# One sign operation of 1536 columns in place of three of 512, in the attention stage of a decoder layer

## The chip, the cores and the metric

The kernel runs on one core of a Trainium2 chip. The metric is the device time of one execution in microseconds, the median of several runs.

## The reference

The reference is a decoder layer of batch 4, 512 tokens and width 512, in fp32: x + attention(layernorm(x)), and then x + ffn(layernorm(x)). The attention has 32 query heads and 8 key and value heads of 16 columns. Its four linear maps use only the signs of their weights, with a scale for each output row.

The part that the change touches is the weights of the ffn. Each of its three matrices is made of a weight w and a mean m:

```
d = w - base
coeff = jnp.mean(jnp.abs(d))
return base + coeff * jnp.sign(d)
```

So three things are needed of each difference d: its sign, element by element, and the mean of its magnitudes over the whole matrix. The ffn is then silu(x W1) * (x W3) times W2, with 1792 inner columns.

## The kernel before

The core runs in stages. The first projects the first batch's tokens. The second, from about 85 to 450 us, is the attention, and all that can be done beside it stands in it too. The third makes the ffn's weights and transposes them, and the last, from about 545 us, is the ffn.

**The attention stage** is written as 32 groups g (4 batches x 8 key heads) of 4 slices kt (tiles of 128 keys), 128 slices in all, numbered 4g + kt. Each engine has its own function for a slice, and the order of the work is written out by hand: on each engine the instructions run in the order of the program, and semaphores tie the engines together.

In a slice TensorE (pe_slice) does, in this order: two of the slice's four transposed score tiles (shifted_scores, L1554), one pair of natural scores of a later group for the maxima (scores, L1538), the piece beside if there is one, another pair of natural scores, the other two transposed scores, and the matmuls that weigh the values with the exps of the slice before (weigh_values, L1564). In slices of kt 1 a transposition of the maxima (L1544) follows.

The transposed scores go to a ring of three PSUM banks (RING3). Each user of the ring waits (ring_free) until the user three places before it has been read: for a score, until its exp is done.

The piece beside (function beside) is work of the next batch: a transposition of tokens in slices 0 to 3 of a batch's 32, pieces of projections (L1445 and L1446) in slices 5, 6, 8, 9, 11, 12, 14, 15, 17, 18, 20 and 21, and a transposition of values in 19. In the first batch all of these come two slices later. In the last batch slices 22, 24, 26 and 28 hold output projections instead.

ScalarE (act_slice) does for each slice: four exps (L1018), with the read of the piece beside between the second and the third (for a projection, L925); in slices of kt 0 a copy of the weighed values (copy_u, L1038), which waits for the value matmuls; and then, from a table by slice, its part of the ffn's weights.

VectorE takes the maxima of the natural scores (L1188), and turns them into a shift (L1196, L1198) that goes into the query slots by DMA (load_shift, L517) before the next group's transposed scores.

**The ffn's weights.** They have 14 tiles e, each with three parts k of 128 x 512 (w1, w3, w2). Buffers wn (three of them) hold w and mn (two) the mean. For tile e, DIFF_AT[e] = 8, 16, ... 112 is the slice in which GpSimd takes the first difference, in place in wn (difference, L799, semaphore fd_ok); the other two come in the next two slices. SIGN_LAG is 2: ScalarE takes the sign of part k in slice DIFF_AT[e] + 2 + k (L1029, semaphore fsgn_ok), into sgn, an int8 tile [128, 14, 3, 512], and the magnitudes of part k, with their sum, in slice DIFF_AT[e] + 5 + k (L1031, semaphore facc_ok), in place in wn. The sync engine loads the next tile into a buffer wn when fsgn_ok and facc_ok have both reached the count of the tile that was in it (load_difference). The signs are next read after slice 123, by full_weights.

So the signs of a tile stand in slices DIFF_AT[e] + 2, + 3 and + 4, which are slices of kt 2, 3 and 0.

Of the kernel before, what the change touches and what calls it, by code (L numbers as in the profile page):

```python
# [11 lines left out]
ACT = mybir.ActivationFunctionType  # L12
# [49 lines left out]
def positive(eng, sem, value):  # L62

    if not isinstance(value, int) or value > 0:
        eng.wait_ge(sem, value)
# [32 lines left out]
def decoder_layer(nc, x, q_w, q_s, k_w, k_s, v_w, v_s, o_w, o_s, w1, m1, w2, m2, w3, m3, out):  # L98
    ctx = ExitStack()

    def sem(name):
        return ctx.enter_context(nc.semaphore(name))
# [47 lines left out]
    wn, mn = stage[0::2], stage[1::2]  # L150
# [40 lines left out]
    with ExitStack() as scope:  # L191
        sb = region(scope)
        sb("below_sgn", [P, 2144])
        sgn = sb("sgn", [P, IT, 3, HID], I8)
# [65 lines left out]
    fd_ok = sem("fd_ok")  # L260
    fsgn_ok = sem("fsgn_ok")
# [119 lines left out]
    def beside(g, kt):  # L381

        b, at = g // KV_HEADS + 1, 4 * (g % KV_HEADS) + kt
        if b == BATCH:
            return ("project", PROJECT_AT.index(at)) if at in PROJECT_AT else None
        at -= LATER[b]
        if XT_AT <= at < XT_AT + KT:
            return "xT", b, at - XT_AT
        for i in range(len(ITEMS)):
            if 0 <= at - ITEM_AT[i] < 2:  # L390
                return "item", b, i, at - ITEM_AT[i]
        if at == VT_AT:
            return "vT", b
        return None
# [12 lines left out]
    def ring_bank(user):  # L407
        return RING3[ring_place[user] % len(RING3)]

    def score_number(g, kt, j):  # L410
        return 16 * g + 4 * kt + J_ORDER.index(j)
# [483 lines left out]
    def _(act):  # L895
# [89 lines left out]
        def beside_out(user):  # L985

            kind, b, *which = user
            bank = ring_bank(user)
            if kind == "xT":
                kt = which[0]  # L990
                act.wait_ge(xT_ok, 4 * b + kt + 1)
                nc.scalar.activation(xn[:, :, kt * P:(kt + 1) * P], BANK[bank].rearrange("p (t c) -> p t c", c=P),
                                     ACT.Copy).then_inc(xe_ok, 1)
            elif kind == "item":
                scale_item(b, which[0], bank, which[1])
            elif kind == "vT":
                values_out(b, bank)


        def hi_attended(b, kt):  # L1000
            act.wait_ge(aT_ok, 4 * b + kt + 1)
            positive(act, o_mm, 4 * b)
            nc.scalar.activation(ah[:, kt, :], an[:, kt, :], ACT.Copy).then_inc(ah_ok, 1)
# [6 lines left out]
        def act_slice(g, kt):  # L1010

            for j in J_ORDER:
                if j == J_ORDER[2] and beside(g, kt):
                    beside_out(beside(g, kt))
                act.wait_ge(t_mm, score_number(g, kt, j) + 1)
                if j == 0:
                    positive(act, pv_mm, 4 * g + kt - 3)
                nc.scalar.activation(probs[kt][:, j, :], BANK[ring_bank(("score", g, kt, j))], ACT.Exp,  # L1018
                                     scale=HEAD_DIM ** -0.5).then_inc(exp_ok, 1)
            if kt == 0 and g > 0:  # L1020
                copy_u(g - 1)
            k = 4 * g + kt - SLICES * (BATCH - 1) - ATTENDED_AT - 1
            if 0 <= k < KT:
                hi_attended(0, k)
            for e in range(IT):
                k = 4 * g + kt - DIFF_AT[e] - SIGN_LAG
                if 0 <= k < 3:
                    act.wait_ge(fd_ok, 3 * e + k + 1)
                    nc.scalar.activation(sgn[:, e, k, :], wn[e % 3][:, k, :], ACT.Sign).then_inc(fsgn_ok, 1)  # L1029
                if 3 <= k < 6:  # L1030
                    nc.scalar.activation(wn[e % 3][:, k - 3, :], wn[e % 3][:, k - 3, :], ACT.Abs,  # L1031
                                         accum_out=dsum[:, k - 3, e:e + 1]).then_inc(facc_ok, 1)

        def copy_u(g):
            act.wait_ge(pv_mm, 4 * g + 4)
            if g >= 2:
                act.wait_ge(u_out[g % 2], 16 * (g // 2))
            nc.scalar.activation(u_sb[g % 2][:], BANK[6], ACT.Copy).then_inc(u_ok, 1)  # L1038

        for g in range(GROUPS):  # L1040
            for kt in range(TT):
                act_slice(g, kt)
# [692 lines left out]
```

## Time and profile before

| | us |
|---|---|
| median of 3 runs | 998.81 |
| lowest and highest of them | 993.24 and 1002.25 |
| the profiled execution | 1002.4 |
| its span in the profile | 1000.6 |

The span reaches from the first to the last instruction; the 1.8 us between it and the execution's time lie around it. In the rows below, PE is TensorE's matmuls, PEld its weight loads, DVE VectorE, ACT ScalarE, POOL GpSimd, and SPq the sync engine's queue that issues the DMAs. "L1029" is line 1029 of the kernel. A row in the order of time merges neighbouring instructions of one line and says how many there are (x2), so its length is that of the group. In brackets stands how long the engine sat idle before it, and which instruction ended that. A weight load's idle time is not a stall of TensorE where matmuls run meanwhile.

### The profile page before, as it was taken

How to read it: one execution, taken by the hardware profiler on the slowest of the kernel's cores; microseconds unless marked ns; L12 is line 12 of the kernel's file. 1: busy time of each engine (PE TensorE's matmuls, PEld its weight loads, DVE VectorE, ACT ScalarE, POOL GpSimd, SP SyncE). 2: the span in 40 equal slices, each digit the busy share in tenths (PEclk: the TensorE clock that was granted, in tenths of full speed). 3: DMA queues.
4: the chain of work that ended last, by engine and by line, in shares of the span. 5: the costliest groups of instructions: out<-in, count | busy, mean ns of one | idle time of the engine just before them, and what ended most of it. 6: DMA issues, size and time to landing. Idle time of an engine off the chain costs nothing.

```text
span 1000.6 us, 14963 instructions
## 1 busy us (share of the span) xinstructions
PE 958.1 (96%) x5030; PEld 624.2 (62%) x5030; DVE 712.1 (71%) x948; ACT 553.4 (55%) x1078; POOL 304.7 (30%) x312
## 2 busy tenths in 40 slices
PE   7899999999999998987999999999999999999997
PEld 6544434443344433333678888888888888888886
DVE  6778898889888897866955588655886558854443
ACT  5468889889988997955842322423223332232220
POOL 4864666467546413445011111011110111101110
PEclk9979999999999998989999999999999999999999
DMA  6435655465545565623830002310023100220001
GB/s 193 122 109 175 206 162 167 138 209 160 165 130 181 164 208 171 202 68 114 278 125 24 1 1 84 124 50 0 0 84 124 49 0 0 84 84 1 0 0 43
DMA packets 75662, 105.06 MB, mean 105 GB/s; under 512 B 9944, under 2 KB 33496, under 8 KB 75608
## 3 DMA queue, kind: packets, MB, share of 16 engines
q1 hardware_dynamic: 74776, 103.26, 32.9%
q0 software_dynamic: 448, 0.46, 0.2%
q8 instruction: 29, 0.48, 0.2%
q10 hardware_dynamic: 384, 0.66, 0.2%
q14 instruction: 25, 0.20, 0.1%
HBM read 74.59 MB, written 28.05 MB: 103 GB/s over the span
## 4 chain that ended last, share of the span: by engine, by line
PE 81%; DVE 6%; ACT 3%; DMA 3%; POOL 3%; issue 3%; SPq 1%; ACTq 0%; DVEq 0%; POOLq 0%
PE psum L1660 15%; PE psum L1661 15%; PE psum L1662 15%; PE psum L1564 9%; PE psum L1554 8%; PE psum L1538 6%; PE psum L1445 3%; DVE nmx L1188 2%; PE psum L1446 2%; PE psum L1650 2%; PE psum L1575 2%; PE psum L1576 1%; ACT probs L1018 1%; DMA q_slot<-shift 1%; PE psum L1434 1%
## 5 line engine op out<-in xcount | busy, mean ns | idle before, releaser
L1188 DVE TENSOR_REDUCE nmx<-psum 128x2 f32<-128x1024 f32 x256 | 304.6, 1220 | 61.0 <-PE psum L1538 58.9
L1018 ACT ACTIVATE probs<-psum 128x512 f32<-128x512 f32 x512 | 270.8, 602 | 47.5 <-PE psum L1554 45.9
L879 POOL CAST dh<-w2T 128x512 fp32r<-128x512 f32 (+1 forms) x56 | 50.7, 906 | 425.9 <-PE psum L1662 393.7
L1660 PE MATMUL psum<-fxh,wh 128*128 128x512 f32 x448 | 175.1, 391 | 2.2 <-DVE wl L1368 2.2
L1661 PE MATMUL psum<-fxl,wh 128*128 128x512 f32 x448 | 175.2, 391 | 0.0
L1662 PE MATMUL psum<-fxh,wl 128*128 128x512 f32 x448 | 174.9, 390 | 0.0
L1554 PE MATMUL psum<-q_slot,k_slot 50*128 50x512 f32 x512 | 151.3, 478 | 15.0 <-ACT probs L1018 5.9
L1554 PEld LDWEIGHTS psum<-q_slot,k_slot 50*128 50x128 f32 x512 | 65.3, 189 | 132.1 <-ACT probs L1018 62.5
L1564 PE MATMUL psum<-probs,v_slot 128*32 128x512 f32 x1024 | 139.8, 619 | 0.0
L1375 DVE TENSOR_TENSOR gate<-gate,psum 128x512 f32<-128x512 f32 x56 | 38.4, 686 | 133.9 <-PE psum L1662 131.6
L1076 ACT ACTIVATE hh<-gate 128x512 fp32r<-128x512 f32 x56 | 35.4, 632 | 162.0 <-DVE gate L1375 162.0
L1073 ACT ACTIVATE gate<-psum 128x512 f32<-128x512 f32 x56 | 33.5, 598 | 164.3 <-PE psum L1662 164.2
L1538 PE MATMUL psum<-k_slot,q_slot 48*128 48x512 f32 x512 | 105.2, 442 | 4.5 <-DVE nmx L1188 3.3
L1660 PEld LDWEIGHTS psum<-fxh,wh 128*128 128x128 f32 x448 | 84.5, 189 | 20.8 <-issue 2.8
L1662 PEld LDWEIGHTS psum<-fxh,wl 128*128 128x128 f32 x448 | 84.5, 189 | 17.7
L1661 PEld LDWEIGHTS psum<-fxl,wh 128*128 128x128 f32 x448 | 84.4, 188 | 17.7
L1660 PE MATMUL psum<-dh,hh 128*128 128x512 f32 x224 | 88.2, 394 | 0.1
L1661 PE MATMUL psum<-dl,hh 128*128 128x512 f32 x224 | 88.2, 394 | 0.0
L1662 PE MATMUL psum<-dh,hl 128*128 128x512 f32 x224 | 87.1, 389 | 0.0
L1538 PEld LDWEIGHTS psum<-k_slot,q_slot 48*128 48x128 f32 x512 | 49.5, 189 | 28.6 <-DVE nmx L1188 15.0
L1377 DVE TENSOR_TENSOR hl<-gate,hh 128x512 fp32r<-128x512 f32 x56 | 38.8, 692 | 39.8 <-ACT hh L1076 39.8
L799 POOL TENSOR_TENSOR stage<-stage 128x512 f32<-128x512 f32 x42 | 53.2, 1280 | 12.5 <-DMA stage<-in_L_ffn_mean_w_dram 12.5
(134 smaller groups left out, 1337.3 us busy)
## 6 DMA issues: line engine op xcount, KB each, us to landing
stage<-in_L_ffn_mean_w_dram SPq DMA_DIRECT2D x84, 256.0 KB, 3.8
q_slot<-q_stack SPq DMA_DIRECT2D x180, 64.0 KB, 2.3
stage<-in_L_ffn_w_dram SPq DMA_DIRECT2D x42, 256.0 KB, 3.8
weighted_values<-u_sb SPq DMA_DIRECT2D x32, 256.0 KB, 2.4
k_slot<-k_stack SPq DMA_DIRECT2D x60, 96.0 KB, 2.4
an<-weighted_values SPq DMA_DIRECT2D x16, 256.0 KB
al<-reciprocals SPq DMA_DIRECT2D x16, 256.0 KB
x<-_attn_hidden_states_dram SPq DMA_DIRECT2D x8, 512.0 KB, 4.2
```

Source lines behind the costliest of these rows:

```text
L799: nc.gpsimd.tensor_tensor(wn[e % 3][:, k, :], wn[e % 3][:, k, :], mn[e % 2][:, k, :], ALU.subtract).then_inc(fd_ok, 1)
L879: nc.gpsimd.tensor_copy(dh[parity][:], w2T[:, bass.ds(src, 1), :].rearrange("p o c -> p (o c)")).then_inc(dh_ok, 1)
L1018: nc.scalar.activation(probs[kt][:, j, :], BANK[ring_bank(("score", g, kt, j))], ACT.Exp, scale=HEAD_DIM ** -0.5).then_inc(exp_ok, 1)
L1188: v.tensor_reduce(column, pair, AX.X, ALU.max, negate=True).then_inc(s_max, 1)
L1375: v.tensor_tensor(gate[:], gate[:], BANK[UP], ALU.mult).then_inc(h_ok, 1)
L1377: v.tensor_tensor(hl[p][:], gate[:], hh[p][:].bitcast(FP32), ALU.subtract).then_inc(hl_ok, 1)
L1538: last = mm(BANK[2 * jj + h], q_slot[s][rows, jj, q * P:(q + 1) * P], k_slot[s][rows, :], start=True, stop=True)
L1554: mm(BANK[ring_bank(("score", g, kt, j))], k_slot[s][rows, kt * P:(kt + 1) * P], q_slot[s][rows, jj, :], start=True, stop=True).then_inc(t ...
L1564: last = mm(psum[32 * j:32 * j + 32, 6, :], v_slot[g % V_SLOTS][:, kt, :], probs[kt][:, j, :], start=(kt == 0), stop=(kt == TT - 1))
L1660: mm(o, lhs_hi, rhs_hi, start=first, stop=False)
L1661: mm(o, lhs_hi, rhs_lo, start=False, stop=False)
L1662: return mm(o, lhs_lo, rhs_hi, start=False, stop=final)
```

## The change

In act_slice the sign of part k is no longer taken in slice DIFF_AT[e] + 2 + k. In slice DIFF_AT[e] + 4, where k is 2, one operation takes the signs of all three parts, 1536 columns of each partition. It waits until all three differences are done, which is the count that the third sign waited for, and it adds 3 to fsgn_ok at once. The magnitudes stay where they were.

```diff
             for e in range(IT):
                 k = 4 * g + kt - DIFF_AT[e] - SIGN_LAG
-                if 0 <= k < 3:
-                    act.wait_ge(fd_ok, 3 * e + k + 1)
-                    nc.scalar.activation(sgn[:, e, k, :], wn[e % 3][:, k, :], ACT.Sign).then_inc(fsgn_ok, 1)
+                if k == 2:
+                    act.wait_ge(fd_ok, 3 * (e + 1))
+                    nc.scalar.activation(sgn[:, e, :, :], wn[e % 3][:], ACT.Sign).then_inc(fsgn_ok, 3)
                 if 3 <= k < 6:
                     nc.scalar.activation(wn[e % 3][:, k - 3, :], wn[e % 3][:, k - 3, :], ACT.Abs,
                                          accum_out=dsum[:, k - 3, e:e + 1]).then_inc(facc_ok, 1)
```

## Rows read from the trace of the kernel before

**Rows 1.** The page, busy time, share of the span and instructions of each engine.

```profile
PE 958.1 (96%) x5030; PEld 624.2 (62%) x5030; DVE 712.1 (71%) x948; ACT 553.4 (55%) x1078; POOL 304.7 (30%) x312
```

**Rows 2.** Line 1029: durations, first and last start.

```profile
L1029 ACT ACTIVATE sgn<-stage x42: 619/632/662, 90.6 to 424.4; 128x512 int8<-128x512 f32 x42
```

**Rows 3.** Stretches: length, busy PE, PEld, DVE, ACT, POOL, then clock, DMA share, GB/s.

```profile
85.00:340.00 255.00, 248.97 (x1614) 110.87 (x1611) 217.37 (x236) 229.64 (x474) 146.50 (x138) 1.00 0.55 168
340.00:450.00 110.00, 99.35 (x561) 38.51 (x558) 87.09 (x95) 89.35 (x183) 38.90 (x38) 0.93 0.53 162
```

**Rows 4.** Waits from 85 to 450 us: us in total, times, longest.

```profile
PEld psum L1554 <- ACT probs L1018: 55.0, 98, 1.7
```

**Rows 5.** ScalarE in order of time, slices 99 to 101.

```profile
368.17 2.06 ACT L1018 ACTIVATE probs<-psum 128x512 f32<-128x512 f32 x4
370.09 0.65 ACT L1029 ACTIVATE sgn<-stage 128x512 int8<-128x512 f32 x1
370.77 2.06 ACT L1018 ACTIVATE probs<-psum 128x512 f32<-128x512 f32 x4
372.98 0.60 ACT L1038 ACTIVATE u_sb<-psum 128x512 f32<-128x512 f32 x1
373.48 0.62 ACT L1029 ACTIVATE sgn<-stage 128x512 int8<-128x512 f32 x1
374.00 2.05 ACT L1018 ACTIVATE probs<-psum 128x512 f32<-128x512 f32 x4
```

**Rows 6.** TensorE in the same slices.

```profile
371.85 1.06 PE L1564 MATMUL psum<-probs,v_slot 128*32 128x512 f32 x8
...
374.64 0.18 PEld L1554 LDWEIGHTS psum<-q_slot,k_slot 50*128 50x128 f32 x1 [0.49 <-ACT probs L1018]
...
375.07 1.06 PE L1564 MATMUL psum<-probs,v_slot 128*32 128x512 f32 x8
```

**Rows 7.** TensorE, a projection piece beside: behind copy and third sign; from 109.34, another slice.

```profile
95.66 1.07 PE L1564 MATMUL psum<-probs,v_slot 128*32 128x512 f32 x8
...
98.93 0.18 PEld L1554 LDWEIGHTS psum<-q_slot,k_slot 50*128 50x128 f32 x1 [0.20 <-ACT probs L1018]
...
99.36 1.07 PE L1564 MATMUL psum<-probs,v_slot 128*32 128x512 f32 x8
...
109.34 1.07 PE L1564 MATMUL psum<-probs,v_slot 128*32 128x512 f32 x8
...
112.80 1.07 PE L1564 MATMUL psum<-probs,v_slot 128*32 128x512 f32 x8
```

**Rows 8.** A tile whose signs wait for GpSimd, in order of time.

```profile
146.83 0.63 ACT L1029 ACTIVATE sgn<-stage 128x512 int8<-128x512 f32 x1 [0.20 <-POOL stage L799]
...
148.68 1.28 POOL L799 TENSOR_TENSOR stage<-stage 128x512 f32<-128x512 f32 x1
...
150.05 0.62 ACT L1029 ACTIVATE sgn<-stage 128x512 int8<-128x512 f32 x1
```

**Rows 9.** ScalarE by form: busy us, mean ns, idle time before it.

```profile
L1029 ACT ACTIVATE sgn<-stage 128x512 int8<-128x512 f32 x42 | 26.7, 636 | 0.5 <-POOL stage L799 0.5
...
L925 ACT ACTIVATE yq<-psum,wstat 128x256 f32<-128x256 f32 x36 | 17.1, 476 | 8.3 <-PE psum L1446 8.0
...
L1031 ACT ACTIVATION_READ_ACCUMULATOR stage<-stage 128x1 f32 x42 | 9.2, 219 | 0.0
...
L925 ACT ACTIVATE yq<-psum,wstat 128x512 f32<-128x512 f32 x6 | 4.1, 684 | 6.9 <-PE psum L1446 6.9
```

**Rows 10.** The sync queue, and TensorE's waits for shift rows.

```profile
374.89 0.60 SPq L563 DMA_DIRECT2D al<-reciprocals  x1
376.73 1.16 SPq L517 DMA_DIRECT2D q_slot<-shift  x2
...
384.74 0.79 PE L1554 MATMUL psum<-q_slot,k_slot 50*128 50x512 f32 x2 [3.19 <-DMA q_slot<-shift]
...
409.92 0.50 PE L1554 MATMUL psum<-q_slot,k_slot 50*128 50x512 f32 x2 [0.56 <-DMA q_slot<-shift]
```

## The prediction

> **What bounds the kernel now.** I read the page's busy shares first: TensorE is busy 96% of the span, ScalarE 55% [rows 1]. That alone would say that ScalarE doesn't matter. The stretches by stage say otherwise. All 42 signs start between 90.6 and 424.4 us [rows 2], in the attention stage. There ScalarE is busy 229.64 of 255 us and later 89.35 of 110 us [rows 3], near TensorE's 248.97 and 99.35. So I went on to the waits of that stage: TensorE's loads for a transposed score (L1554) wait for the exps (L1018) 98 times, 55.0 us in sum [rows 4]. That also counts pauses of the weight loader beside running matmuls; it shows who is tied to whom, not the price.
>
> The timeline shows the loop. In a slice with no other work, ScalarE runs four exps, which go out every 0.49 us, then has a gap, and the next four start 2.60 us after the last (368.17 to 370.77) [rows 5]. The first exp of a slice takes 0.60 and ends at 371.37. It frees the ring's bank for the slice's fourth score, and right behind that score come the value matmuls at 371.85 [rows 6], 0.48 later. They take 1.0 us, the first score of the next slice follows, and its exp closes the loop; these two are the other 1.52 of the 2.60. Only the first exp of each slice is in this loop. The other three are not, nor are the 0.68 us between the last exp's step (370.09, four steps after 368.17) and the next exps. A sign that is taken there, as at 370.09, is free. Whatever holds back the first exp of a slice is paid by everything behind it.
>
> **Part 1, the two early signs removed.** The first two signs of a tile stood at the ends of its slices of kt 2 and 3. Where a slice has no piece beside they took 0.52 (a sign's step, 373.48 to 374.00) of a gap of 0.68 [rows 5]. Where a projection piece runs beside, TensorE needs 3.46 us for a slice (values to values, 109.34 to 112.80 [rows 7]), and ScalarE's work with a sign is shorter: 1.92 for the exps, at most 0.48 for the projection and 0.52 [rows 5, 9], 2.92 in sum. So 26 of the 28 signs cost nothing today and bring nothing. In two places the sign itself waits for GpSimd's difference, 0.5 us together [rows 9], and holds the exps behind it, as at 146.83 [rows 8]. Without it they could start earlier, by the 0.5 us of the two waits at most. But the third sign of the same tile comes at 150.05 and needs a difference that GpSimd starts at 148.68 and ends at 149.96 [rows 8]; being early at 147 only lengthens that wait. I take 0.05 us, 0 to 0.5.
>
> **Part 2, the third sign grows from 512 to 1536 columns.** Its slice is always one of kt 0 in an odd group (12, 20, ... 116), 14 places, and there copy_u stands ahead of it. At 372.98 the copy, at 373.48 the sign, at 374.00 the exps: nothing idle between, and exps to exps is 3.23 us (370.77 to 374.00) in place of 2.60 [rows 5]. Here the sign is already on the path. On TensorE the fourth score's weight load at 374.64 waits for the exp, and the values start at 375.07, 3.22 after those of 371.85 [rows 6]. Any more that the sign takes is added in full.
>
> How much more: the trace has no ScalarE operation of 1536 columns. Scaling a projection takes 684 ns for 512 columns and 476 ns for 256 [rows 9]: 208 ns for 256 columns, 0.81 ns each. The accumulator's read-out (1 column, 219 ns) against the sign (636 ns) gives 0.82 [rows 9]. That is 1024 x 0.81 = 0.83 us more, an operation of about 1.47 us. The upper bound is that nothing of the 0.52 us step from a sign to the next operation is fixed: 2 x 0.52 = 1.04 us more. I take 0.83, because two pairs of rows agree on it and the upper bound is no measurement of a width.
>
> The Trainium skill ("ScalarE: Activation LUTs", What ACT_TABLE_LOAD costs) gives an ACTIVATE 186 ns plus 0.833 ns a column and lets neighbours overlap by 93 ns. By that, the operation would take 1.466 us and the price be 0.853 us; its 613 ns for 512 columns stands against 636 ns in the trace.
>
> Where it is paid. After 8 of the 14 (slices 28, 44, 60, 76, 92, 100, 108, 116) the next slice has nothing beside and the picture is that of rows 5. After the other 6 (12, 20, 36, 52, 68, 84) a projection piece stands in the next slice, which could hide a late exp behind 0.9 us of matmuls. It doesn't: behind the sign of 97.28 the values go from 95.66 to 99.36, 3.70 us, and the fourth score's load at 98.93 waits for an exp, while the same kind of slice after a copy alone takes 3.46 [rows 7]. The cover is used up by the present copy and sign; all the rest is paid. So 14 x 0.83 = 11.6 us before covers.
>
> Two covers. Late in the stage TensorE waits for the shift rows of the next group to land. Behind the sign of 373.48 its matmuls idled 3.19 us for them until 384.74; they were issued at 376.73, right behind a transfer of reciprocals of 374.89 that no sign holds up [rows 10]. If what keeps them eight us on the way are the transfers ahead of them, being issued 0.83 later doesn't make them land later: this place costs 0 (0 to 0.83). Behind the sign of slice 108, at 400.37, the wait is 0.56 us, until 409.92 [rows 10]: this place costs 0.83 less 0.56, 0.27 (0.27 to 0.83). The order of the instructions on the queues, the buffers and GpSimd's differences are as before: the sign waits for the third difference as it did, and behind it on ScalarE stand the same magnitudes and exps. After the stage nothing changes.
>
> **Sum.** 12 x 0.83 = 9.96, plus 0.27, less 0.05: 10.2 us. The profiled execution, 1002.4 us (span 1000.6 and 1.8 around it), would become 1012.6. It lies 3.6 above the median of the runs, 998.81; on the median the same sum gives 1009.0. Ends of the known terms: 14 x 1.04 = 14.6 above, and with the covers 12 x 0.83 + 0.27 less 0.5 = 9.7 below.
>
> **Rivals.**
> A, hidden: the piece beside and the waits for VectorE and DMA cover the longer sign in most places. For it: ScalarE is not the 96% engine, and in the stage TensorE waits for others too. Against: exps to exps is 3.23 and not 2.60 today, so cover is gone before the change. If only the eight bare slices paid, and two of them as above: 6 x 0.83 + 0.27 = 5.3 us, 1004. Wholly hidden: 998.8.
> B, the other side, fewer fixed costs: each tile issues 3 operations of a 0.52 us step now, 1.56 us, and then one of 0.52 + 0.83 = 1.35. That frees 0.21 us of ScalarE a tile, 2.9 us in 14. It decides if ScalarE's total work in the stage (319 of 365 us [rows 3]) sets the pace, averaged over some slices, so that it doesn't matter which slice has the sign. Time 995.9. Against: the signs of kt 2 and 3 have 0.16 us idle behind them [rows 5], and there is no queue of finished scores deeper than three banks to average over. The page's rule named above speaks for this side too: two operations less save 2 x 93 ns a tile, 2.6 us.
> C, dearer: a wide operation with a byte output and rows of 512 costs by the upper bound, and the two DMA waits move along: 14.6 us, 1013.4.
>
> **How the numbers follow.** Forecast (8 to 12 us more) 0.66; A 0.17 (within it wholly hidden 0.05); B 0.07; C 0.10. A measurement of this kernel tells about 1% from no change, 10 us, and the forecast sits on that line. Slower by over 1%: a little over half of the forecast, and C with most of its share, and some scatter: 0.46. Faster by over 1% would need more than B has: 0.03. Within 1%: 0.51. The range has to hold A in part and C: low 1000, high 1014.
>
> **What would show it.** The page should show 14 signs of 128x1536, each 1.45 to 1.49 us. Exps to exps around them should read 4.06 us in place of 3.23, the gaps behind the slices of kt 2 and 3 should be idle for 0.6 us, and their period still 2.60. The matmuls' wait of 3.19 for the shift rows should shrink by about 0.8 and the stage's end move by about 10 us with the stretches behind it unchanged. The prediction is wrong if the slice after the sign keeps its length (A), if slices without a sign get shorter (B), or if the sign takes 1.6 us or more (C).

## The result, and the profile after

The changed kernel takes 1022.26 us (median of 4 runs, 1010.54 to 1026.19), beside 1000.53 for the kernel before: a ratio of 1.018, with an interval of 1.012 to 1.024. Forecast were 1009.0 and a range up to 1014. One of the four runs, 1026.19, counts as slow (over 1.5% above the fastest) and is left out of the ratio; without it the median is 1021.63. The direction and the path of the longer sign are as forecast, the size is not: 18 us by the ratio, 22 by the medians, in place of 10.

The page and the stretches of the changed kernel, against [rows 1, 3]:

```profile
PE 971.7 (95%) x5030; PEld 628.9 (62%) x5030; DVE 712.7 (70%) x948; ACT 552.2 (54%) x1050; POOL 304.6 (30%) x312
...
85.00:340.00 255.00, 244.21 (x1507) 108.36 (x1503) 203.18 (x221) 212.54 (x422) 140.59 (x132) 0.95 0.51 156
340.00:455.00 115.00, 107.79 (x617) 42.08 (x609) 91.89 (x95) 97.55 (x194) 35.59 (x37) 0.93 0.57 177
```

ScalarE's busy time fell by 1.2 us, and TensorE's rose by 13.6 with the same 5030 matmuls. That can't come from waiting: waiting is idle time. The column behind the busy times says what it is. From 85 to 340 us the granted clock was 1.00 before and is 0.95 now.

The sign itself, the line 1029 of the changed kernel, answers to [rows 2, 9]:

```profile
L1029 ACT ACTIVATE sgn<-stage x14: 1474/1476/1483, 96.1 to 442.3; 128x1536 int8<-128x1536 f32 x14
```

1476 ns, 844 more than the median of 632 before (forecast: 1.47 us and 0.83 more). By the figures of the Trainium skill ("ScalarE: Activation LUTs", What ACT_TABLE_LOAD costs), 186 ns plus 0.833 ns a column, it would be 1466, an estimate, and the trace agrees within 1%. The sign's step, from its start to that of the next exps, is 1.37 us. The bare place of rows 5 and 6 (tile 11) now reads so, ScalarE first and then TensorE:

```profile
387.96 2.06 ACT L1018 ACTIVATE probs<-psum 128x512 f32<-128x512 f32 x4 [0.54 <-PE psum L1554]
390.57 2.07 ACT L1018 ACTIVATE probs<-psum 128x512 f32<-128x512 f32 x4 [0.55 <-PE psum L1554]
392.78 0.60 ACT L1038 ACTIVATE u_sb<-psum 128x512 f32<-128x512 f32 x1
393.28 1.48 ACT L1029 ACTIVATE sgn<-stage 128x1536 int8<-128x1536 f32 x1
394.65 2.05 ACT L1018 ACTIVATE probs<-psum 128x512 f32<-128x512 f32 x4
```

```profile
391.65 1.07 PE L1564 MATMUL psum<-probs,v_slot 128*32 128x512 f32 x8
...
395.29 0.49 PE L1554 MATMUL psum<-q_slot,k_slot 50*128 50x512 f32 x1 [1.01 <-ACT probs L1018]
395.71 1.07 PE L1564 MATMUL psum<-probs,v_slot 128*32 128x512 f32 x8
```

From the exps of one slice to those of the next it is still 2.61 us in the slice without a sign (387.96 to 390.57), with 0.55 idle where a sign had stood, and 4.08 with copy and sign (3.23 before). From value matmuls to value matmuls it is 4.06 (3.22 before). With a projection piece beside, at tile 0, it is 4.56 (3.70 in [rows 7]):

```profile
94.47 1.07 PE L1564 MATMUL psum<-probs,v_slot 128*32 128x512 f32 x8
...
98.11 0.99 PE L1554 MATMUL psum<-q_slot,k_slot 50*128 50x512 f32 x2 [0.37 <-ACT probs L1018]
99.03 1.07 PE L1564 MATMUL psum<-probs,v_slot 128*32 128x512 f32 x8
```

Up to here each step is as forecast. The rest shows behind tile 4. First the fourth score behind its third sign in the kernel before, then two rows of the changed kernel: the same score, and the value matmuls two slices later.

```profile
202.03 0.50 PE L1554 MATMUL psum<-q_slot,k_slot 50*128 50x512 f32 x1 [0.58 <-ACT probs L1018]
```

```profile
206.29 0.50 PE L1554 MATMUL psum<-q_slot,k_slot 50*128 50x512 f32 x1 [1.45 <-ACT probs L1018]
...
212.50 1.93 PE L1564 MATMUL psum<-probs,v_slot 128*32 128x512 f32 x8
```

The stretches around it, first of the kernel before, where the clock stays at 1.00, then of the changed one:

```profile
200.00:205.00 5.00, 4.40 (x30) 1.99 (x27) 3.99 (x6) 4.84 (x11) 4.20 (x5) 1.00 0.85 258
205.00:210.00 5.00, 5.00 (x38) 2.62 (x40) 3.93 (x5) 4.12 (x10) 0.07 (x1) 1.00 0.74 191
```

```profile
200.00:205.00 5.00, 4.83 (x35) 2.43 (x31) 3.84 (x5) 4.18 (x8) 2.52 (x5) 1.00 0.70 216
205.00:210.00 5.00, 3.71 (x17) 1.58 (x18) 2.87 (x5) 4.27 (x9) 2.78 (x3) 0.75 0.79 256
210.00:215.00 5.00, 5.00 (x23) 2.13 (x22) 1.92 (x2) 2.38 (x7) 0.00 (x0) 0.57 0.60 178
```

TensorE idles 1.45 us, and 1 us behind it the granted clock goes from 1.00 to 0.50, from 2.4 to 1.2 GHz. Until it returns, eight value matmuls take 1.93 us in place of 1.07. In stretches of 1 us, six such drops come behind wide signs of the profiled execution: from 152 (tile 2), 207 (tile 4), 313 (tile 8), 371 (tile 10), 419 (tile 12) and 446 us (tile 13). They begin up to about 2 us behind the fourth score and last 3 to 14 us each. In the kernel before the same score follows on 0.4 to 0.6 us of idle time at five of the eight bare places and on less at the others, and no drop begins between 85 and 383 us.

The starts of copy_u, one for each group, are good marks for where the 19.2 us of span come from, since both kernels have them:

| marks around | before, us | after, us | more, us | of it clock, us |
|---|---|---|---|---|
| tiles 0, 1, 3, 6, 7, 9: each | | | 0.8 to 0.9 | 0 |
| tile 5 | | | 0.46 | |
| tile 4 | 13.20 | 16.96 | 3.76 | about 2.9 |
| tiles 2, 8 and 10 | | | 2.49, 6.56, 3.16 | about 1.6, 5.7, 2.3 |
| tile 11 | 15.96 | 12.10 | -3.86 | |
| tiles 12 and 13 | | | 2.18, 2.26 | about 1.3, 1.4 |

"Of it clock" is what is left over 0.85, an estimate. Fourteen signs at 0.84 to 0.86 are some 12 us; the drops are some 15 us; the first marks, ahead of any sign, stand 1.1 us earlier than before; and at tile 11 the kernel before loses time that the changed one doesn't: its wait of 3.19 us for the shift rows and a clock at 0.50 from 383 to 391 us [rows 10]. After the last mark both kernels take the same, 531.9 and 531.7 us.

### The profile page after: what moved, and what is told of

Same layout as the page of the kernel before. It is cut to its first block, busy times and chain, and to the rows that moved or that the text cites. A ratio compares the mean times of both kernels' runs of the same rounds, so it can differ in the third digit from the quotient of the medians.

```text
span 1019.8 us, 14949 instructions
## 1 busy us (share of the span) xinstructions
PE 971.7 (95%) x5030; PEld 628.9 (62%) x5030; DVE 712.7 (70%) x948; ACT 552.2 (54%) x1050; POOL 304.6 (30%) x312
## 4 chain that ended last, share of the span: by engine, by line
PE 84%; ACT 5%; DVE 4%; POOL 3%; issue 3%; DMA 1%; SPq 0%; ACTq 0%; DVEq 0%; POOLq 0%
PE psum L1660 15%; PE psum L1661 15%; PE psum L1662 15%; PE psum L1564 10%; PE psum L1554 10%; PE psum L1538 6%; PE psum L1445 3%; PE psum L1650 2%; ACT sgn L1029 2%; PE psum L1446 2%; ACT probs L1018 2%; PE psum L1575 2%; PE psum L1576 1%; DVE nmx L1188 1%; PE psum L1434 1%
## 5 line engine op out<-in xcount | busy, mean ns | idle before, releaser
L1554 PE MATMUL psum<-q_slot,k_slot 50*128 50x512 f32 x512 | 155.8, 489 | 20.5 <-ACT probs L1018 15.3
L1554 PEld LDWEIGHTS psum<-q_slot,k_slot 50*128 50x128 f32 x512 | 66.9, 193 | 142.1 <-ACT probs L1018 74.5
L1564 PE MATMUL psum<-probs,v_slot 128*32 128x512 f32 x1024 | 145.1, 640 | 0.0
L1538 PE MATMUL psum<-k_slot,q_slot 48*128 48x512 f32 x512 | 108.0, 454 | 3.7 <-DVE nmx L1188 2.6
L799 POOL TENSOR_TENSOR stage<-stage 128x512 f32<-128x512 f32 x42 | 53.2, 1280 | 11.6 <-DMA stage<-in_L_ffn_mean_w_dram 11.6
```

The costliest lines, as they stand in the source:

```text
L799: nc.gpsimd.tensor_tensor(wn[e % 3][:, k, :], wn[e % 3][:, k, :], mn[e % 2][:, k, :], ALU.subtract).then_inc(fd_ok, 1)
L1538: last = mm(BANK[2 * jj + h], q_slot[s][rows, jj, q * P:(q + 1) * P], k_slot[s][rows, :], start=True, stop=True)
L1554: mm(BANK[ring_bank(("score", g, kt, j))], k_slot[s][rows, kt * P:(kt + 1) * P], q_slot[s][rows, jj, :], start=True, stop=True).then_inc(t ...
L1564: last = mm(psum[32 * j:32 * j + 32, 6, :], v_slot[g % V_SLOTS][:, kt, :], probs[kt][:, j, :], start=(kt == 0), stop=(kt == TT - 1))
```

## The experiments

Each ratio below is taken against runs of the kernel before made beside the experiment (three rounds, medians 1000.58, 999.52 and 1001.88 us). Where an edit adds lines, the numbers of the lines behind it move, so that L1555, L1558 or L1559 can be the scores' L1554.

The working theory after the result: (1) the longer sign is paid in full at nearly every place, about 11 us; (2) the idle time of TensorE behind it makes its clock fall, and the drops cost about as much again. Rivals: the width of the operation itself is bad (for GpSimd, the memory, the DMAs); or something else that varies from run to run.

**The changed kernel again.**

> The changed kernel once more, beside the others. Theory 'idle and clock': the sign's extra 0.85 us is paid at about 13 of 14 places (11 us), and the rest of the loss is TensorE's granted clock, which falls to half for 3 to 13 us behind some of the bare slices, so that the time varies from run to run with the clock: 1010 to 1026 us, ratio 1.01 to 1.025, and a run with a mean clock of 0.98 is 10 us faster than one with 0.967. Rival 'something else is dearer' (GpSimd, DMA): the same time whatever the clock is.

1020.45 us, ratio 1.021 (1.016 to 1.027). Its runs, with the mean clock of each: 1017.16 (0.973), 1018.97 (0.972), 1021.93 (0.971), 1028.76 (0.959). Of the first four runs one had 0.982, as high as the kernel before has on average (63 runs: 0.982 and 1001.3 us), and it took 1010.54: what the sum of the prediction gives. The time goes with the clock. The profile of this repetition has only three drops behind wide signs, from 154, 209 and 318 us (tiles 2, 4 and 8). After the same waits at the other five, the longest of them 1.33 us, none came:

```profile
442.35 0.50 PE L1554 MATMUL psum<-q_slot,k_slot 50*128 50x512 f32 x1 [1.33 <-ACT probs L1018]
...
442.00:452.00 10.00, 8.95 (x52) 3.78 (x54) 6.38 (x8) 7.38 (x17) 2.66 (x2) 1.00 0.37 111
```

**The idle time filled.** In the bare slices behind a wide sign TensorE repeats the third score while it waits, so that it has the same waits for ScalarE but is not idle:

```diff
...
+            for _ in range(again):
+                mm(BANK[ring_bank(("score", g, kt, j))], k_slot[s][rows, kt * P:(kt + 1) * P], q_slot[s][rows, jj, :],
+                   start=True, stop=True)
             mm(BANK[ring_bank(("score", g, kt, j))], k_slot[s][rows, kt * P:(kt + 1) * P], q_slot[s][rows, jj, :],
...
```

> Changed kernel, and in the 8 bare slices behind a wide sign TensorE repeats the third score's matmul four times (about 0.9 us of work that changes nothing) while it waits for ScalarE. Theory 'idle and clock': the places still cost 0.85 us each, 11 us in all, but the waits of 0.8 to 1.7 us shrink by 0.9 and the clock no longer falls behind a sign; 1009 to 1013, 8 to 12 us better than the changed kernel where its clock falls. Rival 'the clock is no cause': extra work in front of the fourth score can only cost; the same time as the changed kernel or up to 2 us more, and half-clock stretches where they were.

1014.62 us, ratio 1.012 (1.008 to 1.015), mean clock of the runs 0.974 to 0.984. Adding 32 useless matmuls made the changed kernel some 6 us faster, a little less than the 8 to 12 expected. But 4 repeats left 0.5 us idle behind tiles 4, 8 and 12 (the next expectation names 11 and 13, a misreading), and drops from 313 us (tile 8) and 415 us (tile 12) remained; there was also one behind tile 1, where no repeat stands, and one at a wait of 1.29 us for shift rows. So the number was fitted to each place (7 in tile 2, 6 in 4, 8 and 13, 5 in 11, 4 in 6, 10 and 12):

> As the run with four repeats, but as many as the idle time behind each bare sign has room for: 7 in tile 2, 6 in 4, 8 and 13, 5 in 11, 4 in the other three. The waits of 0.5 us that were left behind tiles 4, 8, 11 and 13 should go. Theory 'idle and clock': the sign's own 11 us stay, the clock falls no more behind the bare signs; mean clock 0.98 or more, ratio 1.009 to 1.012, and better than the changed kernel by 7 us or more. Rival 'the gain of the first filled kernel was chance': ratio near 1.018 again, or worse by the added matmuls.

1012.37 us in 12 runs, ratio 1.009 (1.005 to 1.013), mean clock 0.983 over the runs, as the kernel before. In its profile no drop begins between 85 and 364 us; two of some 3 us remain, behind tiles 10 and 12, where no wait of TensorE near them was over 0.41 us. The stretches around tile 4, and the whole stage up to 340 us, of this kernel:

```profile
200.00:205.00 5.00, 5.00 (x36) 2.87 (x36) 4.01 (x4) 3.90 (x8) 3.04 (x3) 1.00 0.60 172
205.00:210.00 5.00, 4.94 (x32) 2.28 (x30) 3.72 (x4) 4.81 (x9) 4.40 (x4) 1.00 0.85 220
210.00:215.00 5.00, 4.99 (x36) 2.58 (x33) 3.34 (x5) 4.30 (x11) 0.30 (x2) 1.00 0.68 216
...
85.00:340.00 255.00, 248.16 (x1588) 112.66 (x1580) 209.48 (x227) 220.15 (x435) 143.32 (x134) 1.00 0.56 165
```

And the two copies around tile 4, first of the changed kernel, then of this one:

```profile
203.78 0.60 ACT L1038 ACTIVATE u_sb<-psum 128x512 f32<-128x512 f32 x1
...
220.74 0.60 ACT L1038 ACTIVATE u_sb<-psum 128x512 f32<-128x512 f32 x1 [0.15 <-PE psum L1564]
```

```profile
206.21 0.60 ACT L1038 ACTIVATE u_sb<-psum 128x512 f32<-128x512 f32 x1
...
220.26 0.60 ACT L1038 ACTIVATE u_sb<-psum 128x512 f32<-128x512 f32 x1
```

16.96 us there, 14.05 here, 13.20 before: the sign's 0.85 stays and the rest is gone. With the ratios, 1.018 and 1.021 unfilled and 1.009 filled, this gives the split. About 1% is the length of the sign, and the other 1% is TensorE's clock behind the idle time.

**By kind of place.** The wide sign only in the six tiles with a piece behind, or only in the eight bare ones:

```diff
...
+                wide = e in (0, 1, 3, 5, 7, 9)
+                if wide and k == 2:
+                    act.wait_ge(fd_ok, 3 * (e + 1))
+                    nc.scalar.activation(sgn[:, e, :, :], wn[e % 3][:], ACT.Sign).then_inc(fsgn_ok, 3)
+                if not wide and 0 <= k < 3:
...
```

> The one sign of 1536 columns only at the 6 tiles whose next slice has a piece beside (tiles 0, 1, 3, 5, 7, 9); the other 8 keep three signs. Theory 'idle and clock': 6 x 0.85 = 5.1 us more than before and no clock lost behind a sign, because TensorE waits under 0.8 us there: ratio 1.004 to 1.006. Rival A of the prediction (the piece hides the longer sign): ratio 1.000. Rival 'any wide sign drops the clock': 5 us plus a share of 6 in 14 of the clock's loss, ratio 1.01.

1004.07 us, ratio 1.002 (1.000 to 1.004); by the medians 3.5 us. That is less than the 1.004 to 1.006 expected, and the interval reaches 1.000, so the time alone doesn't refute the rival that the pieces hide the sign. The marks do: they show 0.84 to 0.86 paid at tiles 0, 3, 7 and 9. At tile 5 it is 0.46, and what hides the other 0.4 is a wait for VectorE further on and not the piece. It was 0.73 us before and is 0.33 here, first the kernel before and then this one:

```profile
235.25 0.51 PE L1538 MATMUL psum<-k_slot,q_slot 48*128 48x512 f32 x2 [0.73 <-DVE nmx L1188]
```

```profile
241.99 0.50 PE L1542 MATMUL psum<-k_slot,q_slot 48*128 48x512 f32 x2 [0.33 <-DVE nmx L1192]
```

At tile 1 the marks show 6.48 us: the clock fell there, after only 0.74 us idle:

```profile
126.24 1.18 PE L1558 MATMUL psum<-q_slot,k_slot 50*128 50x512 f32 x2 [0.74 <-ACT probs L1018]
...
130.00:140.00 10.00, 10.00 (x42) 5.29 (x40) 5.31 (x11) 4.81 (x10) 1.03 (x2) 0.50 0.62 187
```

The expectation that nothing is lost to the clock here was wrong for this execution. Over the 10 runs the mean clock was 0.984, so it is no rule. Tile 1 is the one of the six whose next slice (21) holds the transposition of values and not a projection: TensorE idles 0.74 to 0.76 us there behind a wide sign and 0.33 to 0.37 at the other five. Its clock fell in this profile and in that with four repeats, and not in those of the changed kernel, its repetition and the fitted one.

> The one sign of 1536 columns only at the 8 tiles whose next slice is bare (tiles 2, 4, 6, 8, 10 to 13); the other 6 keep three signs. Theory 'idle and clock': 8 x 0.85 = 6.8 us less one place hidden by a DMA wait, and nearly all of the clock's loss, since the idle times over 0.8 us are there: mean clock about 0.97, ratio 1.01 to 1.016. Together with the six it should give the changed kernel's loss. Rival 'each tile adds the same': 8 in 14 of the whole change, ratio 1.011, and a clock between the two kernels'.

1014.29 us, ratio 1.012 (1.007 to 1.018), mean clock 0.975. The eight bare places carry most of the loss and most of the clock's share of it. By the ratios the two kernels together lose 1.4%, beside 1.8 and 2.1% for the changed kernel in its two rounds; the intervals are too wide to say whether something is missing.

**Place or width.** Three signs of 512 columns, all in the slice of kt 0:

```diff
...
+                if k == 2:
+                    for part in range(3):
+                        act.wait_ge(fd_ok, 3 * e + part + 1)
+                        nc.scalar.activation(sgn[:, e, part, :], wn[e % 3][:, part, :], ACT.Sign).then_inc(fsgn_ok, 1)
```

> Three signs of 512 columns, but all three in the slice of kt 0 where the one of 1536 stands. Theory 'place and idle': what counts is how long ScalarE holds the next exps; three steps of 0.52 are 1.56 us against 1.37, so 1.04 us more a tile than the kernel before, 13 to 14 us, and 2.6 more than the changed kernel, with at least as much of the clock lost: ratio 1.02 to 1.028. Rival 'width': operations of 512 columns are harmless as before; ratio under 1.005.

1028.63 us, ratio 1.026 (1.019 to 1.034), mean clock 0.965. Exps to exps at tile 11:

```profile
391.85 2.06 ACT L1018 ACTIVATE probs<-psum 128x512 f32<-128x512 f32 x4 [0.54 <-PE psum L1555]
394.06 0.60 ACT L1039 ACTIVATE u_sb<-psum 128x512 f32<-128x512 f32 x1
394.56 1.66 ACT L1030 ACTIVATE sgn<-stage 128x512 int8<-128x512 f32 x3
396.12 2.05 ACT L1018 ACTIVATE probs<-psum 128x512 f32<-128x512 f32 x4
```

4.27 us, 0.19 over the wide sign. So the merging does save ScalarE 0.19 us a tile, near the 0.21 of rival B; it is worth nothing beside the place. Narrow operations in that place do the same harm, and the rival 'width' falls.

**The wide sign one slice earlier**, in the gap of kt 3 (k == 1 in place of k == 2):

> The one sign of 1536 columns is taken one slice earlier, at the end of the tile's slice of kt 3, where no copy stands ahead of it and a bare slice has a gap of 0.68 us. Theory 'place': it needs 1.37 us of a gap of 0.68, so 0.69 at the bare places and less beside a projection piece, and the 0.52 of the third sign at kt 0 is saved at all 14: 0 to 3 us faster or slower than the kernel before, ratio 0.997 to 1.003, with few or no half-clock stretches behind signs. Rival 'width itself': an operation of 1536 columns hurts wherever it stands, ratio 1.01 or more.

1009.69 us, ratio 1.009 (1.006 to 1.012): 9 us in place of -3 to 3. The expectation missed, and the number is nearly that of its rival 'width itself'.

```profile
355.58 2.06 ACT L1018 ACTIVATE probs<-psum 128x512 f32<-128x512 f32 x4 [0.53 <-PE psum L1554]
357.51 1.51 ACT L1029 ACTIVATE sgn<-stage 128x1536 int8<-128x1536 f32 x1
358.88 2.09 ACT L1018 ACTIVATE probs<-psum 128x512 f32<-128x512 f32 x4
361.11 0.60 ACT L1038 ACTIVATE u_sb<-psum 128x512 f32<-128x512 f32 x1
361.60 1.57 ACT L1018 ACTIVATE probs<-psum 128x512 f32<-128x512 f32 x3
```

The slice with the sign is 3.30 (0.69 over 2.61), the one with the copy 2.72 (0.51 under 3.23), as expected. But where a piece stands behind, the marks show 0.74 added (tile 3) and only 0.24 saved: [rows 7] had said so, 3.70 against 3.46. With 0.2 to 0.3 at eight tiles, 0.5 at six and 3.9 us of waits for GpSimd's third difference (4 times) it is 9 us. I had taken 0.52 for saved at all 14. This is an account and not a measurement, and it has no term for the clock: 3.37 of the 3.9 us are one wait, at tile 2, TensorE idles 4.25 us behind it, and the clock is at half from 151 us on. The steps of ScalarE are those of the theory 'place', so nothing here needs the width as a cause.

```profile
152.54 0.79 PE L1554 MATMUL psum<-q_slot,k_slot 50*128 50x512 f32 x1 [4.25 <-ACT probs L1018]
...
151.00:161.00 10.00, 8.46 (x34) 3.39 (x34) 3.14 (x5) 7.00 (x14) 5.19 (x4) 0.50 0.07 21
```

**No sign at kt 0.** Two of 768 columns at kt 2 and 3; or three of 512, each one slice earlier:

```diff
...
+                if 0 <= k < 2:
+                    c = slice(768 * k, 768 * (k + 1))
+                    act.wait_ge(fd_ok, 3 * e + 2 + k)
...
```

```diff
...
+                if -1 <= k < 2:
+                    act.wait_ge(fd_ok, 3 * e + k + 2)
...
```

> Two signs of 768 columns, at the ends of the tile's slices of kt 2 and 3, and none at kt 0. Each takes 0.73 us of a gap of 0.68 in a bare slice. Theory 'place': 0.05 us twice a tile against 0.52 saved at kt 0, so 0.4 us a tile, 5 to 6 us less than before, but the first of them needs the second difference already in its slice, and GpSimd is sometimes late (3.9 us in the run with the wide sign at kt 3), which takes 2 to 4 us back: 0.996 to 1.000. Rival 'TensorE or VectorE bounds those places anyway': ratio 1.000, or above by the waits for GpSimd.

> Three signs of 512 columns as before, each one slice earlier (kt 1, 2 and 3; one slice behind its difference in place of two). Theory 'place': 0.52 us at kt 0 is saved at 14 places, 7 us, and the three others stand in gaps; waits for GpSimd's differences take 2 to 4 us back. Ratio 0.993 to 0.998. Rival as in the other run: 1.000 or above.

1003.65 us, ratio 1.003 (1.000 to 1.007), and 1003.66, ratio 1.003 (1.000 to 1.006). Neither gains: both expectations missed, and both rivals' numbers came. In each of the two, six signs wait for GpSimd, 6.0 us in sum, which is more than the 2 to 4 expected. In the second the marks show 0.25 saved at a tile with a projection piece and 0.1 to 0.5 at a bare one, and its longest wait stands in a slice where the exps are held for it:

```profile
140.99 0.63 ACT L1029 ACTIVATE sgn<-stage 128x512 int8<-128x512 f32 x1 [3.04 <-POOL stage L799]
```

The mean clock is 0.978, beside 0.983 for the kernel before in that round; in the first it is 0.981. The last version is early only where GpSimd is in time:

```diff
...
+                early = 1 if e not in (2, 6, 11, 12, 13) else 0
+                if 0 <= k + early < 3:
+                    part = k + early
...
```

> Three signs of 512 columns one slice earlier (kt 1, 2, 3), but only in the 9 tiles where GpSimd's differences were in time or nearly so; tiles 2, 6, 11, 12 and 13 as in the kernel before. From the marks of the copies in the run with all tiles early: 0.25 us gained at each tile with a piece behind it and 0.47 at each bare one, 6 x 0.25 + 3 x 0.47 = 2.9 us: ratio 0.996 to 0.998, if the clock stays at 0.98. Rival 'TensorE's clock takes it back': ratio 1.000 or above with a mean clock of 0.978 or less.

998.67 us, ratio 0.998 (0.995 to 1.001), mean clock 0.984. By size it is what was expected; that it is faster than the kernel before is likely and not shown, since the interval reaches 1. It beats the changed kernel by 2%.

**The drops counted.** The profiles of all kernels that bear on it, at the eight bare places: TensorE's idle time before the fourth score, and the drops that begin at it or up to about 2 us behind it.

| kernel | idle time, us | drops |
|---|---|---|
| before | up to 0.59 | 0 of 8 |
| wide sign at the six | up to 0.59 | 0 of 8 |
| changed | 0.79 to 1.69 | 6 of 8 |
| changed, again | 0.86 to 1.68 | 3 of 8 |
| wide sign at the eight | 0.88 to 1.70 | 4 of 8 |
| three signs at kt 0 | 0.95 to 1.64 | 8 of 8 |
| changed, four repeats | up to 0.53 | 2 of 8 |
| changed, fitted repeats | up to 0.41 | 2 of 8 |

So it is 21 of 32 with the long waits and 4 of 32 without them, one profile for each kernel.

## Why the prediction was wrong

- **The loop and what is on it**: right. 2.60 us without anything, a sign free at kt 2 and 3, and the third on the path; the pieces beside hide nothing of it. Two details were off: behind tile 1 (slice 20) stands the transposition of values and not a projection piece, and at tile 5 a wait for VectorE hides 0.4 of the 0.85 us.
- **The operation's length**: right, 844 ns more against 0.83 us.
- **The two early signs**: right. Tile 2's wait for GpSimd went and its third sign waited for GpSimd instead (0.27 us); the marks give 0.4 us gained in the group before it, which is inside the 0 to 0.5.
- **The two covers**: not as argued. The long wait for the shift rows at tile 11 was not a fixed cover of 0.83; in the changed kernel it wasn't there at all, and in nine of the ten other profiled kernels these two marks are closer by 0.7 to 3.9 us than in the kernel before (in the tenth, three signs one slice earlier, they are 1.1 us further apart). It came and went with the execution. The wait of 0.56 us behind tile 12 was not there in the changed kernel either. Neither cover hid anything, and that the sum without them (11.6) lies within 2 us of the sum with them is no merit of theirs.
- **The step that failed**: "Any more that the sign takes is added in full" was taken for the whole price. The sum priced TensorE's idle time at its length. It had no term for what TensorE does after it: waits for the exps of 0.8 to 1.7 us in place of 0.6 at most, and a clock at half for 3 to 14 us behind six of eight bare places, some 15 us in sum in that execution by the marks. The runs with the idle time filled show what the term is worth over many executions: 1.018 to 1.021 without the filling, 1.009 with it, some 10 us. The row for it was at hand: the wait of 3.19 us in [rows 10] ends at 384.74, the clock of the kernel before stands at 0.50 from 384 to 390 us, and I read that wait as a cover only.
- **The range** ended at the sum of the known terms (1014) plus nothing for an unknown one on the same side.

The filled version is within the forecast (1012.37, ratio 1.009), which is why I call the priced part of the mechanism right and the missing clock the error.

## What to carry to other kernels

Ask of a merged operation where its time will stand, before what it saves: two of the three signs stood in gaps and were free, the third stood in the one slice without a gap and cost its 0.52 us. Merging moved the work of the free two to the third, which cost 0.85 us more a time for 0.19 us of ScalarE saved. Where TensorE waits in a loop with another engine, price a longer wait at more than its length: look in the trace of before whether the granted clock falls behind its longest idle times, and add that. In the profile, a TensorE that is busier with the same number of matmuls, and a granted clock that went down in the stage, is the mark of it.

## What the runs showed of the hardware that wasn't expected

The granted clock can halve soon after short idle times of TensorE in an otherwise busy stage. The length of the one idle time doesn't decide: behind the wide signs of the changed kernel's profile the clock fell after 1.69, 1.45, 1.44, 1.33, 0.87 and 0.79 us and not after 1.03 and 1.01, nor after a wait of 1.24 us for VectorE at 145.22. In the same kernel's second profile it didn't fall after 1.33 and 1.31. In other kernels it fell after 0.74 and after 0.41. What else counts stays open. The cost varies from run to run: the same changed kernel took 1010.54 us at a mean clock of 0.982 and 1028.76 at 0.959. And matmuls whose results nobody needs can pay for themselves: 42 of them, fitted into the waits, made the changed kernel about 1% faster.
